# Two cross-attention layers with heads taken in pairs: 64-row scores, GpSimd clips and divides

## The reference, cut to what matters

```python
# layer 0: 16 heads of 16 dimensions, scores clipped at +-10000
q = LN(x) @ Wq + bq; k = ctx @ Wk + bk; v = ctx @ Wv + bv
p = softmax(clip(q_h @ k_h.T * 0.25, -1e4, 1e4))        # per head h
x = x + tanh(g_xattn[0]) * (concat_h(p @ v_h) @ Wo + bo)

# layer 1: 16 heads of 64 dimensions, low-rank terms added to the weights,
# 371 context tokens, and 4 image tokens with keys and values of their own
p = softmax(q_h @ k_h.T * 0.125)                         # 371 keys
o = p @ v_h + softmax(q_h @ k_image.T * 0.125) @ v_image # 4 keys
x = x + tanh(g_xattn[1]) * (concat_h(o) @ Wo + bo)
```

## Time and profile before

| | |
|---|---|
| three runs | 1277.67 us median, 1271.22 to 1278.12 |
| the profiled execution, first to last instruction | 1277.4 us |
| layer 0 attention, its steady part and prologue | about 46 to 296 us |
| layer 0 experts and mixing | about 300 to 615 us |
| layer 1 attention | about 622 to 993 us |
| layer 1 experts | about 993 to 1277 us |
| busy over the whole span | PE 83%, DVE 74%, ACT 44%, POOL 21% |

### The profile page before, as it was taken

The page is one execution under the profiler, slowest core; times in us unless marked ns, Lnnn a source line. Parts: engine busy times, 40 slices in busy tenths (PEclk is TensorE's granted clock), DMA queues, the critical chain, the costliest instruction groups (busy, mean ns, idle before and its releaser), DMA issues.

```text
span 1277.4 us, 23029 instructions
## 1 busy us (share of the span) xinstructions
PE 1066.5 (83%) x7860; PEld 746.0 (58%) x7860; DVE 948.8 (74%) x2024; ACT 567.6 (44%) x1276; POOL 268.6 (21%) x303
## 2 busy tenths in 40 slices
PE   0688888882979999854688988998897699999997
PEld 0577777771634555643367877777776455455553
DVE  5588888897398888697567777777776667776775
ACT  3366666672433343441455556555555233222220
POOL 1422222202245563001000000000000013433331
PEclk9899999995699999896799999999998699999999
DMA  5000000001112122320000000000000231112100
GB/s 190 1 2 2 1 0 0 0 1 66 64 48 84 58 96 67 110 71 28 6 1 2 2 2 1 1 0 1 1 1 1 100 129 64 64 64 72 70 1 29
DMA packets 9935, 47.82 MB, mean 37 GB/s; under 512 B 1513, under 2 KB 3313, under 8 KB 6930
## 3 DMA queue, kind: packets, MB, share of 16 engines
q1 hardware_dynamic: 9874, 47.03, 10.7%
HBM read 45.92 MB, written 1.11 MB: 37 GB/s over the span
## 4 chain that ended last, share of the span: by engine, by line
PE 33%; DVE 30%; issue 20%; ACT 9%; POOL 5%; DMA 2%; DVEq 1%; ACTq 0%; POOLq 0%
PE pb L1119 8%; PE pb L1134 7%; POOL qz L1227 5%; DVE ST L844 4%; DVE ST L855 3%; DVE nm L850 3%; PE pb L640 2%; PE pb L613 2%; PE pb L597 2%; DVE ST L847 2%; ACT ST L728 2%; PE pb L1424 2%; PE pb L576 1%; ACT V L711 1%; PE pb L570 1%
## 5 line engine op out<-in xcount | busy, mean ns | idle before, releaser
L1119 PE MATMUL pb<-xT,KT 128*128 128x448 f16 x1248 | 244.2, 354 | 2.7 <-DVE qz L1197 2.7
L1227 POOL TENSOR_TENSOR qz<-qz,Z 128x448 f32<-128x448 f32 x128 | 169.1, 1331 | 286.8 <-ACT qz L1166 197.5
L1119 PEld LDWEIGHTS pb<-xT,KT 128*128 128x128 f16 x1248 | 121.6, 98 | 119.6 <-DVE qz L1197 5.8
L613 PE MATMUL pb<-KT,qz 128*112 128x375 f16 (+1 forms) x768 | 171.8, 334 | 3.2 <-POOL qz L921 2.1
L640 PE MATMUL pb<-V,ST 125*112 125x32 f16 (+1 forms) x1536 | 127.0, 214 | 53.2 <-DVE ST L855 52.9
L1134 PE MATMUL pb<-V,KT 128*128 128x448 f16 x816 | 162.6, 357 | 8.9 <-DVE V L1206 8.9
L640 PEld LDWEIGHTS pb<-V,ST 125*112 125x112 f16 x1536 | 109.9, 133 | 71.3 <-DVE ST L855 47.2
L736 ACT ACTIVATE ST<-pb 125x336 f16<-125x336 f32 x256 | 113.6, 444 | 45.1 <-PE pb L623 42.5
L855 DVE SCALAR_TENSOR_TENSOR ST<-pb,ST 125x336 f16<-125x336 f32 x256 | 127.7, 499 | 6.0 <-ACT ST L736 5.4
L1134 PEld LDWEIGHTS pb<-V,KT 128*128 128x128 f16 x816 | 80.3, 99 | 86.3 <-DVE V L1206 10.5
L623 PE MATMUL pb<-identf,ST 112*125 112x112 f32 x768 | 125.8, 273 | 1.6 <-ACT ST L728 1.6
(11 more groups left out here) (196 smaller groups left out, 1594.0 us busy)
## 6 DMA issues: line engine op xcount, KB each, us to landing
ST<-in_moe SPq DMA_DIRECT2D x9, 1536.0 KB, 7.8
ST<-in_moe SPq DMA_DIRECT2D x8, 1024.0 KB, 6.8
Z<-wd_scratch SPq DMA_DIRECT2D x16, 448.0 KB, 4.4
ST<-in_ctxT SPq DMA_DIRECT2D x4, 750.0 KB, 4.9
ST<-in_gens SPq DMA_DIRECT2D x2, 768.0 KB, 4.7
ST<-in_lora SPq DMA_DIRECT2D x2, 624.0 KB, 8.7
ST<-in_w1q SPq DMA_DIRECT2D x1, 1024.0 KB
ST<-in_w1k SPq DMA_DIRECT2D x1, 1024.0 KB
```

The costliest lines, as they stand in the source:

```text
L613: mm = pe.matmul(SB_[st % 2][0:S, 0:L.keys], qz[:, bs % 2, qa, h, :], kT[bs % 2][qb][:, h // L.per_tile, 0:L.keys], start=(n == 0), stop=( ...
L1119: mm = pe.matmul(banks[m % len(banks)][:, 0:HT], MW[:, es % 2, qa, c:c + 128], xT[:, qb, k, half * HT:(half + 1) * HT], start=(i == 0), st ...
L1227: pool.tensor_tensor(tile, tile, wdB[:, es % 2, half * HT:(half + 1) * HT], ALU.mult)\
```

## The change

Heads go in pairs (`NP` = 8 steps for a batch). `SB_[0]` and `SB_[1]` now hold the two heads of one pair and are one tile `SP2`; `TB_` likewise is `TP2`. One instruction serves both heads in the reduction of layer 1, in hi, in lo and in the patch. The two heads of a pair lie on different halves of the 128 rows, and their score matmuls take 64 rows each and alternate. In layer 0 that takes four scaled copies of q (`qv`, one for each head modulo 4) in place of the masks on POOL; ACT and DVE write them with a per-partition scale `par`. The second clip of layer 0 goes from DVE to POOL. Normalise reads both halves in one reduction; in layer 1 its division goes to POOL. The units of both layers get other places, and turn(p - 1) now directly follows the exponentials of the same pair.

```diff
-NORM_LAG = (3, 3)
+NORM_LAG = 2
         if index == 0:
-            at = {0: 0, 1: 3, 2: 5, 3: 7, 4: 9, 5: 11}
-            out_at = {0: 5, 1: 8}
+            at = {0: 1, 1: 3, 2: 5, 3: 7, 4: 9, 5: 11}
+            out_at = {0: 5, 1: 13}
         else:
-            at = {n: min(15, n) for n in range(len(self.front))}
-            out_at = {0: 4, 1: 5, 2: 11}
+            at = dict(enumerate((1, 1, 2, 3, 3, 4, 5, 6, 7, 7, 8, 12, 13, 13, 14, 15, 15)))
+            out_at = {0: 5, 1: 9, 2: 11}
+        order = [0, 4, 1, 5, 2, 6, 3, 7]
+        self.order = list(range(H)) if index else order + [8 + h for h in order]
+        self.pairs = [self.order[2 * p:2 * p + 2] for p in range(NP)]
...
+            def scores(bv, bs, p):
...
+                if st >= 1:
+                    pe.wait_ge(s["mx_done0"] if l == 0 else s["exp_done1"], 2 * i)
                 for n, (qa, qb) in enumerate(PARTS):
-                    mm = pe.matmul(SB_[st % 2][0:S, 0:L.keys], qz[:, bs % 2, qa, h, :],
-                                   kT[bs % 2][qb][:, h // L.per_tile, 0:L.keys], start=(n == 0), stop=(n == 2))
+                    for j, h in enumerate(L.pairs[p]):
+                        if l == 0:
+                            t, r = h // 8, slice(64 * (h % 8 // 4), 64 * (h % 8 // 4) + 64)
+                            q = qv[r, bs % 2, h % 4, qa, t, :]
+                        else:
+                            t, r = h // 2, slice(64 * (h % 2), 64 * (h % 2) + 64)
+                            q = qz[r, bs % 2, qa, h, :]
+                        mm = pe.matmul(SB_[j][0:S, 0:L.keys], q, kT[bs % 2][qb][r, t, 0:L.keys],
+                                       start=(n == 0), stop=(n == 2))
...
+            def turn(i, st):
+                if l == 0:
+                    pe.wait_ge(s["exp_done0"], 2 * i + 2)
+                else:
+                    pe.wait_ge(s["ipa_patch1"], i + 1)
+                if st >= 1:
+                    pe.wait_ge(s[f"lo_done{l}"], i)
...                                                       # PE, batch():
+                for p in range(NP):
+                    if bs or p >= 1:
+                        turn(bv * NP + p - 1, bs * NP + p - 1)
+                    ...                                    # units of head 2p
+                    if p >= 2:
+                        weigh(bv, bs, p - 2)
+                    ...                                    # units of head 2p + 1
+                    if p < NP - 1:
+                        scores(bv, bs, p + 1)
...                                                       # ACT
                 if u[0] == "q" and l == 0:
+                    for v in range(VAR):
+                        x = act.activation(qv[:, bs % 2, v, 0, :, :], ..., ACT.Copy, scale=par[:, v:v + 1])
...
+                for p in range(NP):
+                    if bs or p >= 1:
+                        hi(bv * NP + p - 1, bs * NP + p - 1)
+                    for j in range(2):
+                        exps(bv, bs, p, j)
+                        ...                                # units of head 2p + j
...                                                       # DVE
+                    for j in range(2):
+                        dve.tensor_scalar(SC[:, st % 2, j, :], SB_[j][0:S, 0:L.keys], -CLAMP, CLAMP, ALU.max, ALU.min,
+                                          accum_out=nm[:, c + j:c + j + 1]).then_inc(s["mx_done0"], 1)
                     return
-                dve.tensor_reduce(nm[:, st % 4:st % 4 + 1], src, AX.X, ALU.max, negate=True)\
+                dve.tensor_reduce(nm[:, c:c + 2], SP2[0:S, :, 0:L.keys], AX.X, ALU.max, negate=True)\
...
-                dve.tensor_copy(ob, halves[:, :, 0, :]).then_inc(s[f"halves{l}"], 1)
-                dve.tensor_tensor(ob, ob, halves[:, :, 1, :], ALU.add).then_inc(s[f"halves{l}"], 1)
-                dve.scalar_tensor_tensor(ob, ob, OS if l else 1.0, ...)
+                dve.tensor_reduce(ob, halves, AX.X, ALU.add).then_inc(s[f"halves{l}"], 1)
+                if l:
+                    return
+                dve.tensor_tensor(ob, ob, ...rinv..., ALU.mult).then_inc(s["o_rd0"], 1)
...                                                       # POOL, layer 0 (the masks are gone)
+                for i in range(B * NP):
+                    for j in range(2):
+                        pool.wait_ge(s["mx_done0"], 2 * i + j + 1)
+                        pool.tensor_scalar(SC[:, i % 2, j, :], SC[:, i % 2, j, :], CLAMP, None, ALU.min)
...                                                       # POOL, layer 1: patch of a pair, and
+            def divide(bv, g):
+                pool.wait_ge(s["halves1"], group + 1)
+                pool.tensor_tensor(ob, ob, ...rinv..., ALU.mult).then_inc(s["o_rd1"], 1)
```

More of the change, by code:

```diff
@@ L39 @@
 OS = 16.0
+NP = H // 2
+VAR = 4
 SQ, DEG = 2, 8
@@ L671, in attention_tensor @@
             batch("last", B - 1, B - 1)
-            for i in range(B * H - 2, B * H):
-                turn(i, i)
-                weigh(B - 1, B - 1, i - 1 - (B - 1) * H)
-            weigh(B - 1, B - 1, H - 1)
+            turn(B * NP - 1, B * NP - 1)
+            weigh(B - 1, B - 1, NP - 2)
+            weigh(B - 1, B - 1, NP - 1)
             for _, kind, u, n, ns, _ in tail_units(L):
@@ L765, in attention_scalar @@
             batch("last", B - 1, B - 1)
-            for i in range(B * H - 2, B * H):
-                hi(i, i)
+            hi(B * NP - 1, B * NP - 1)
             for _, kind, u, n, ns, nh in tail_units(L):
@@ L878, in batch @@
+                if l:
+                    return
+                dve.wait_ge(s["halves0"], group + 1)
+                dve.wait_ge(s["r_done0"], group + 1)
+                dve.tensor_tensor(ob, ob, bc(rinv[:, heads].unsqueeze(2), [S, L.grouped, L.dim]), ALU.mult)\
+                   .then_inc(s["o_rd0"], 1)
             def batch(where, bv, bs):
                 todo = unit_numbers(L, where, bv, bs)
[L880 to L896 removed]
@@ new lines, in batch @@
+                for p in range(NP):
+                    maxima(bv, bs, p)
+                    if bs or p >= 1:
+                        lo(bv * NP + p - 1, bs * NP + p - 1)
+                    for j in range(2):
+                        for hh, kind, u, n, ns, nh in todo:
+                            if hh == 2 * p + j:
+                                d = 1 if kind == "front" else -1
+                                unit(kind, u, n, ns, nh, bv + d, bs + d)
+                                if u[0] == "i":
+                                    ipa_rest(bv + d, bs + d)
+                        for g in range(L.groups) if j == 0 else ():
+                            at = (g + 1) * L.grouped // 2 - 1 + NORM_LAG
+                            if at == p:
+                                normalise(bv, bs, g)
+                            elif at == p + NP and bs:
+                                normalise(bv - 1, bs - 1, g)
@@ L907, in attention_vector @@
             batch("last", B - 1, B - 1)
-            for i in range(B * H - 2, B * H):
-                lo(i, i)
+            lo(B * NP - 1, B * NP - 1)
             normalise(B - 1, B - 1, L.groups - 1)
@@ L925, in attention_gpsimd @@
-                masks(0, 0)
-                masks(1, 1)
-                with pool.Fori(1, B // 2) as r:
-                    b = r * 2
-                    masks(b, 2)
-                    masks(b + 1, 3)
-                return
+                for i in range(B * NP):
+                    for j in range(2):
+                        pool.wait_ge(s["mx_done0"], 2 * i + j + 1)
+                        pool.tensor_scalar(SC[:, i % 2, j, :], SC[:, i % 2, j, :], CLAMP, None, ALU.min)\
+                            .then_inc(s["clip_done0"], 1)
@@ L941, in patches @@
                         .then_inc(s["ipa_patch1"], 1)
+                    if bs and p == NORM_LAG - 1:
+                        divide(bv - 1, L.groups - 1)
+                    elif p > NORM_LAG and (p - NORM_LAG) % 2:
+                        divide(bv, (p - NORM_LAG - 1) // 2)
             patches(0, 0)
```

230 lines of the change are left out of this document (104 added, 126 removed).

## The result

The changed kernel is slower: 1323.6 us (median of 4 runs, 1314.8 to 1327.8) against 1277.9 us (1271.2 to 1280.0), a ratio of 1.035 with the interval [1.031, 1.040]. The forecast was 1236. In the profiled execution the span goes from 1277.4 to 1320.2 us.

A forecast was written before the change was run, and what follows sets the result against it. The prediction took layer 0 as bound by DVE and layer 1 by PE. Its sum was 1277.4 - 15 (layer 0) - 26 (layer 1) = 1236 us, with range 1210 to 1272 and the forecast's own range 1222 to 1250.

The forecast's parts named there:

- The clip on POOL: Layer 0's second clip moved to POOL: taken as 0.5 us for 375 columns, upper end 1.15 us.
- The price for the path: Layer 0: if POOL's clip costs 1.15 us, a batch takes 5.7 us more.
- Rival B: Layer 0: POOL's clip costs 1.15 us, +5.7 us a batch, total 1279, no change; chance 0.10.
- The clock: Layer 0: 0.5 us a batch for switches and clock together, raising the walked 28.1 to 28.6.
- Rival C: Layer 0: PE's clock falls to 1.2 GHz, 39 us a batch, total 1314; half the layer gives 1275; chance 0.12.
- The loop of layer 0: Exponentials, transposes, then hi in order: 3.05 us a plain pair, 28.6 a batch, -15 us for the layer.
- the pair's scores: Score matmuls of two heads side by side: 0.48 us a pair; next transposes within 0.5 to 0.65 us.
- The division on POOL: Layer 1's normalise division on POOL: 0.84 us, a step or more ahead of its reader, costing nothing.
- the prediction's signs: Profile checks, including POOL's clip about 0.5 us, layer 0's clock at least 0.90, DVE busy about 22 us a batch.
- Layer 1: Bound by PE; a batch falls from 44.2 to 40.8 us, -26 us for the layer.
- the factor 7.5: Both layers: a microsecond a batch is worth some 7.5 us a layer; of 8 batches, first and last are partial.

The follow-up runs named there:

- the kernel with both edits: Changed kernel with layer 0's second clip back on DVE and each pair's layer 0 score matmuls made twice: 1258.3 us, ratio 0.981 to the kernel before.

## Why the prediction was wrong, point by point

**The clip on POOL, the step that failed.** The text says "It has one input, so I take 0.5". It took 1146 ns, the upper end of its own bound (1.15), and between 1143 and 1149 in all 128 cases, so it is not a matter of what runs beside it. The lower number joined a 292 ns select of 128 columns with a 200 ns instruction of 4 columns: two points of other operations, both short. The row nearest in length was the multiplication, 1331 ns for 448 columns, 3.0 ns a column; the clip's 1146 for 375 is 3.1. The Trainium skill (GPSIMD Engine Reference, Engine selection) calls GpSimd about twice as slow as VectorE for two inputs and roughly at line rate for one; this trace disagrees for the clip, which costs as much per column as the operation with two. The price for the path, 5.7 us a batch, was right: measured 34.9 - 29.0 = 5.9 at 0.95 and 1.00 of the clock. In the total it is 49 us (1307.1 against 1258.3, both with doubled scores; 1323.6 against 1274.9, both without), of which layer 0 has 58.7 and 41.9; that the totals agree owes something to layer 1's low stretch. Rival B had this duration, at a price of 43 us and a chance of 0.10.

**The clock, left at 0.5 us a batch together with the switches.** With POOL's clip in place a batch goes from 34.9 at 0.95 to between 37.2 and 38.7 at 0.62 to 0.70: 2.3 to 3.8. In layer 0 the doubled scores gave back 7.9 us beside POOL's clip and 24.7 beside DVE's, in the total 16 each time. Rival C had the whole layer at the low level and PE as its bound, 39 us a batch. The clock was low for a part of each batch only. The last full batch was at the low level throughout, and there PE does set the pace, 32.2 busy of 32.9 us, where 28.3 were enough in the single run with doubled scores:

```profile
305.90:338.75 32.85, 32.23 (x204) 25.54 (x204) 16.87 (x45) 16.33 (x41) 18.05 (x16) 0.50 0.01 1
```

**Two rivals at once.** B gave 1279 and C with half of the layer 1275, each about no change; added to each other they give 1236 + 43 + 39 = 1318, near the 1324 measured. By the runs the two are 49 + 16 = 65 of the 88 us missing, and 22 are left in the kernel with both edits (1258.3 against 1236), so the nearness of 1318 is partly luck. I had added each to the forecast and never to the other, and so the range ended at 1272. Nor need they be independent: the waits on PE were what spoke for C, and POOL's longer clip adds to them. That link is argued, not shown, since the clock stayed at 0.73 with the clip on DVE.

**The loop of layer 0.** Walked 3.05 us for a plain pair and 28.6 for the batch. With the clips on DVE a pair with a v unit takes 2.90 us where the clock is high, and with doubled scores, at the full clock, the batch takes 29.0. The walk stands; hi (730 ns for 0.73), lo (857 for 0.87) and the pair's scores (0.61 to the next transposes, inside 0.5 to 0.65) do too. The division on POOL took 612 ns, where I had 840. Two of the prediction's signs failed beside B's: the clock of layer 0 was to stay at or above 0.90, and DVE was busy for 20 us of a batch, not 22.

**Layer 1, right in the batch and wrong in the sum.** 40.7 against 40.8 forecast. The term that was mis-sized is the factor 7.5. Five distances between outputs shrank, four by 3.6 us and the one with the low clock by 0.5. The last full batch went from 32.2 to 33.2 us and what follows it from 18.9 to 20.9: where no units stand between the pairs PE waits for the exponentials.

```profile
994.16 0.68 PE L627 MATMUL sp<-KT,qz 64*112 64x371 f16 x6 [1.38 <-ACT ST L760]
...
997.60 0.68 PE L627 MATMUL sp<-KT,qz 64*112 64x371 f16 x6 [1.25 <-ACT ST L760]
```

These are 3.44 us a pair in that last batch of the changed kernel, with PE waiting 1.3 of them. What stands before the first output gave 3.8. Together 4 x 3.6 + 0.5 + 3.8 - 0.9 - 2.0 = 15.8, as measured. Some 6 of the 10 us that are missing are the clock's, and not the factor's: with the clip on DVE, and the same layer 1, it takes 325.4 us, for the time to the first output is 68.2 in place of 70.2, the fifth distance 40.7 in place of 43.8 and the end 19.9 in place of 20.9. There the gain is 21.9 us, a factor of 6.1 on the 3.6 of a batch. In layer 0 of the best version batches are 1.6 us shorter than before (30.6 to 29.0), and the layer by 8.9 (248.0 to 239.1), a factor of 5.5. But the single run of that kernel has 235.8, a factor of 7.6; its time to the first output is 53.0 us at 1.00 where the other's is 56.4 at 0.91. So in layer 0 the factor is not shown to be wrong.

**What stays open.** Why the clock falls where it does. Doubled scores went with a higher clock in every pair of runs above (0.68 to 0.95, 0.78 to 1.00, 0.69 to 0.82). But the version without a second clip holds 1.00 with PE busy for 22.6 of 25.8 us, and the one with the clip on DVE gets 0.78 at 28.6 of 30.7, so the busy share of the profile does not order them: it also rises where each matmul takes longer. Nor is it the mix of work: both have the same transposes and matmuls.

## What to carry to other kernels

Price an operation that no row shows by the nearest row in size and type on the same engine; a kinship of form ("it has one input") is a guess, and the upper end should decide where the instruction is on the loop's path. When a change ties engines more tightly and moves work onto a slow one, add the rivals that feed each other, a longer instruction and the clock of an engine that waits for it, before setting the range. Count the gain for a batch once for each steady batch, and walk the first and the last apart: they have other work in them.

## What the runs showed of the chip that I had not expected

- More matmuls made the kernel faster, twice: 1323.6 to 1307.1 us and 1274.9 to 1258.3, with 384 extra matmuls of 64 rows whose results are written over with the same values. In both the granted clock of layer 0 rose (0.65 to 0.86, 0.73 to 0.96), and with it layer 0 fell by 7.9 and 24.7 us.
- The same clip of 112x375 f32 in SBUF costs 1146 ns on POOL and 0.61 us for two on DVE, between three and four times less. In the kernel before it took DVE 487 ns on average: between 50 and 300 us 356 ns in the 106 cases with POOL idle, and 1067 ns in the 21 with POOL's masks beside it. The clip from PSUM and lo were no slower there (534 and 493 ns beside the masks, 539 and 499 without).
- The changed kernel with the second clips back on DVE and the scores of layer 0 doubled beats both kernels: 1258.3 us, 0.981 [0.976, 0.986] of the kernel before.
